# Squaring the half-angle sines on three engines instead of two, and four small evictions of VectorE moved

## What is computed

```
q, k, v = x @ Wq.T + bq, x @ Wk.T + bk, x @ Wv.T + bv       # 16 heads of 8
f(z)    = [cos(z @ proj / sqrt(8)), sin(z @ proj / sqrt(8))] / sqrt(128)
kv      = sum over tokens of f(k) * v                        # per head
x       = layernorm(x + (f(q) @ kv) @ Wo.T + bo)
p       = softmax(x @ Wr + br), the two largest kept and scaled to sum 1
x       = layernorm(x + sum over the two experts of p_e * (relu(x @ W1e + b1e) @ W2e + b2e))
```

## Time and profile before

| | |
|---|---|
| time, median of 3 runs | 525.64 us (525.46 to 525.82) |
| the profiled execution's own time | 526.61 us |
| its span, first to last instruction | 524.8 us |
| PE busy (matmul) | 475.4 us, 91% |
| DVE busy | 414.2 us, 79% |
| POOL busy | 393.5 us, 75% |
| ACT busy | 370.9 us, 71% |
| the chain that ended last | PE 64%, POOL 13%, issue 6%, DVE 6% |

### The profile page before, as it was taken

One profiled execution on the slowest core, in us unless ns is written; L12 is line 12 of the kernel. 1 busy time (PEld: TensorE's weight loads), 2 busy tenths in 40 slices (PEclk: granted clock), 3 DMA queues, 4 the chain that ended last, 5 costly groups with the idle time before them and its releaser, 6 DMA issues.

```text
span 524.8 us, 12192 instructions
## 1 busy us (share of the span) xinstructions
PE 475.4 (91%) x3739; PEld 277.5 (53%) x3739; DVE 414.2 (79%) x920; ACT 370.9 (71%) x505; POOL 393.5 (75%) x463
## 2 busy tenths in 40 slices
PE   5799999999999999999999998888999999999713
PEld 3343343343344344344344343338999989999701
DVE  4868979979979978988988887567678977777554
ACT  3797888797887888788788787585555555555235
POOL 2383398798888889889779779985777788687654
PEclk9999999999999999999999999899999999999957
DMA  4563154153154154143234221032222333222194
GB/s 102 174 201 122 27 156 126 56 161 122 45 157 162 37 146 153 39 137 137 67 116 141 62 62 47 1 82 58 63 64 73 89 108 94 65 80 59 36 326 156
DMA packets 44740, 53.94 MB, mean 103 GB/s; under 512 B 8563, under 2 KB 25237, under 8 KB 44677
## 3 DMA queue, kind: packets, MB, share of 16 engines
q1 hardware_dynamic: 39728, 43.82, 28.2%
q0 software_dynamic: 4320, 8.95, 5.1%
q10 hardware_dynamic: 628, 0.38, 0.3%
HBM read 33.09 MB, written 20.04 MB: 101 GB/s over the span
## 4 chain that ended last, share of the span: by engine, by line
PE 64%; POOL 13%; issue 6%; DVE 6%; DMA 3%; SPq 3%; ACT 2%; DVEq 0%; POOLq 0%; ACTq 0%
PE misc L643 11%; PE ang L795 10%; PE ang L804 10%; PE ang L592 8%; PE misc L612 7%; POOL rows_s L1489 5%; PE ang L579 5%; PE ang L584 5%; POOL feats L1464 3%; DVE turns L1077 2%; PE misc L531 1%; POOL rstd L1482 1%; ACT feats L883 1%; DMA feats<-expert_dram 1%; PE misc L658 1%
## 5 line engine op out<-in xcount | busy, mean ns | idle before, releaser
L1077 DVE TENSOR_SCALAR turns<-ang 128x1024 f16<-128x1024 f32 x128 | 156.1, 1220 | 44.2 <-PE ang L584 27.1
L882 ACT ACTIVATE feats<-ang 128x1024 f32<-128x1024 f32 x128 | 131.2, 1025 | 62.3 <-PE ang L592 61.6
L1464 POOL TENSOR_TENSOR feats<-feats 128x1024 f32<-128x1024 f32 x56 | 106.8, 1908 | 58.2 <-ACT feats L883 57.7
L883 ACT ACTIVATE feats<-ang 128x1024 f32<-128x1024 f32 x128 | 131.2, 1025 | 0.0
L1085 DVE TENSOR_TENSOR feats<-feats 128x1024 f32<-128x1024 f32 x72 | 92.8, 1289 | 0.6 <-ACT feats L883 0.6
L1633 POOL DMA_INDIRECT routed_dram<-rows_s,slots x64 | 76.2, 1190 | 18.9 <-issue 18.3
L1663 POOL DMA_INDIRECT expert_dram<-feats x71 | 69.9, 985 | 24.5 <-DVE feats L1388 15.5
L592 PE MATMUL ang<-turns,negi 128*128 128x512 f16 x256 | 77.8, 386 | 10.5 <-DVE turns L1077 10.4
L795 PE MATMUL ang<-feats 128*128 128x128 f32 x568 | 76.1, 277 | 3.9 <-DVE feats L1340 3.0
L953 ACT ACTIVATE feats<-experts 128x644 f32 x71 | 52.5, 739 | 34.2 <-DVE feats L1388 27.0
L804 PE MATMUL ang<-experts,feats 128*128 x568 | 75.6, 276 | 0.4 <-DVE feats L1348 0.4
(11 more groups left out here) (199 smaller groups left out, 551.6 us busy)
## 6 DMA issues: line engine op xcount, KB each, us to landing
stk<-parts_dram SPq DMA_DIRECT2D x126, 128.0 KB, 2.7
parts_dram<-parts SPq DMA_DIRECT2D x16, 512.0 KB, 3.2
feats<-routed_dram SPq DMA_DIRECT2D x72, 65.5 KB
experts<-ffn_W SPq DMA_DIRECT2D x16, 256.0 KB, 3.2
feats<-expert_dram SPq DMA_DIRECT2D x16, 256.0 KB, 5.3
out<-feats SPq DMA_DIRECT2D x8, 256.0 KB, 2.1
x_all<-attn_x SPq DMA_DIRECT2D x7, 256.0 KB, 5.1
expert_dram<-feats POOLq DMA_INDIRECT x71
```

The source lines that it names most:

```text
L882: act.activation(f[:, 0, :], a, ACT.Sin, scale=TWO_PI)
L883: act.activation(f[:, 1, :], a, ACT.Sin, scale=TWO_PI / 2).then_inc(s["sines"], 1)
L1077: dve.tensor_scalar(turns[:, u % 2, :], ang[:, slot(ph, u), :], MAGIC, -MAGIC, ALU.add, ALU.add)\
L1464: pool.tensor_tensor(f, f, f, ALU.mult).then_inc(s["sq_p"], 1)
```

## The change

Eight of the 16 squares of a sequence go to DVE (units 0, 2, 4, 5, 6, 10, 13, 15), four to POOL (1, 3, 8, 12) and four to ACT (7, 9, 11, 14). In the diff the first `square` is ACT's and the second DVE's. ACT squares unit `u - 1` behind the sines of unit `u`, so unit 7 in step 8, 9 in step 10, 11 in step 12 and 14 in step 15, with its activation function Square on `feats` in place. Units 4, 6 and 10 leave POOL for DVE; units 7, 9, 11 and 14 leave DVE for ACT. On DVE, `kv_evac` moves from the end of step 12 to just behind its rounding, and `take_ranks` and `move_base` follow it there, ahead of the square of unit 10. The list of POOL's scatters and PE's `ranks` are not touched by the diff.

```diff
-POOL_SQ = (1, 3, 4, 6, 8, 10, 12)
+POOL_SQ = (1, 3, 8, 12)
+ACT_SQ = (7, 9, 11, 14)
...
+DVE_SQ = tuple(u for u in range(UNITS) if u not in POOL_SQ + ACT_SQ)
...
-def before(u, pool):
+def before(u, whose):
 
-    return sum((x in POOL_SQ) == pool for x in range(u))
+    return sum(x in whose for x in range(u))
...
             def squared(b, u):
 
-                wait(pe, "sq_v", UNITS - len(POOL_SQ), b, before(u + 1, False))
-                wait(pe, "sq_p", len(POOL_SQ), b, before(u + 1, True))
+                wait(pe, "sq_v", len(DVE_SQ), b, before(u + 1, DVE_SQ))
+                wait(pe, "sq_p", len(POOL_SQ), b, before(u + 1, POOL_SQ))
+                wait(pe, "sq_a", len(ACT_SQ), b, before(u + 1, ACT_SQ))
...
+            def square(b, u):
+                if u % UNITS not in ACT_SQ:
+                    return
+                wait(act, "sines", UNITS, b, u + 1)
+                f = feats[:, u % HALF, 1, :]
+                act.activation(f, f, ACT.Square).then_inc(s["sq_a"], 1)
...
                     sines(b, ph, u)
+                    if not (first and u == 0):
+                        square(b, u - 1)
...
             def square(b, u):
-                if u % UNITS in POOL_SQ:
+                if u % UNITS not in DVE_SQ:
                     return
...
-            BEFORE_ROUND = ((6, moments), (10, take_logits), (13, move_base))
-            AFTER_ROUND = ((5, residual), (10, largest))
-            AFTER_SQUARE = ((5, statistics), (10, which), (12, take_ranks), (13, slot_numbers))
+            BEFORE_ROUND = ((6, moments), (10, take_logits))
+            AFTER_ROUND = ((5, residual), (10, largest), (12, take_ranks), (12, move_base))
+            AFTER_SQUARE = ((5, statistics), (10, which), (13, slot_numbers))
...
                     if u == 11:
                         kvT_evac(b)
+                    if u == 12:
+                        kv_evac(b)
...
-                    if u == 12:
-                        kv_evac(b)
```

More of the change, by code:

```diff
@@ L249, in build @@
             "raw_T", "raw_ev", "pad_ok", "setup", "sel_0", "sel_ok", "sel_mm", "sel_ev",
-            "angles", "rounded", "reduced", "sines", "sq_v", "sq_p",
+            "angles", "rounded", "reduced", "sines", "sq_v", "sq_p", "sq_a",
             "xT_mm", "xT_ev", "q_mm", "q_ev", "k_mm", "k_ev", "v_mm", "v_ev", "split", "parts_out",
@@ L940, in body @@
                     sines(b, ph, u)
+                    if not (first and u == 0):
+                        square(b, u - 1)
             sequences(body)
+            square(BATCH, -1)
             act.activation(warm[:, :], zero_t[:, :], ACT.Sigmoid)
```

## The result

The changed kernel takes **512.11 us** (median of 4 runs, 511.84 to 513.27) against 525.73 us of the kernel before in the same comparison (525.46 to 529.32, 4 runs): ratio 0.973, 95% interval 0.9685 to 0.9774, a gain of 13.6 us. Forecast were 514.6 us and a gain of 11.0, with a range of 511.5 to 520.5; the measured time lies 0.6 us inside its lower end.

A forecast was written before the change was run, and what follows sets the result against it. PE was taken to bound the middle sequences, with waits for DVE's roundings and POOL to win. Gains 0.9 (first) + 5.4 (middle) + 4.7 (last) = 11.0 us, from 525.64 to 514.6 us; range 511.5 to 520.5.

The forecast's parts named there:

- the first sequence: Step 12 of the first sequence: gain 0.9 us, its wait of 1.14 less 0.2 by which DVE's chain stays late.
- the middle ones: Six middle sequences: 0.9 us each from step 12, 5.4 in all; a middle sequence was to take 40.2 us.
- What can be won: Middle sequences: PE is the bound, so without less work for PE only its idle 1.12 us a sequence can be won.
- Step 12: With unit 9's square on ACT, DVE rounds unit 12 in time and PE's reduction starts earlier: 0.9 us a sequence.
- The walk of what is late next: Step 12 behind the rounding: kv_pad, slot_m and base were to be ready for the first product, with 0.15 us to spare.
- ACT at no cost: ACT's four squares at about 1.0 us each cost PE nothing; unit 11's sines, the tightest place, have 0.8 us to spare.
- The normalised rows: Steps 6 to 8: DVE's added square delays POOL's normalising, so PE's 0.25 us wait stays; bounds -0.3 and +0.4 a sequence.
- The exclusive port of the Trainium skill: DVE and POOL lock the shared port by whole instructions: squares of units 4 and 5 each stop L1489 1.2 us; 2.4 less gain.
- The last sequence: POOL's chain loses three squares, 5.7 us, less 1.0 taken for delay by DVE's squares: the end comes 4.7 us earlier.
- The end: At the change to Sigmoid, ACT's square of unit 14 is covered by the rows from memory: cost nothing, uncovered 1.0 once.
- No table is loaded for Square: Rival on ACT: a table load for each square, eight a sequence, 10.3 us, making the kernel some 580 us; chance 0.06.
- The wait did not move: Rival in step 12: kv_pad and base, or ACT's unit 11, become late instead; 6.3 us go, 520.9 us; chance 0.06.

The follow-up runs named there:

- run 2: The kernel before with the square of unit 9 alone moved from DVE to ACT, DVE's order as before: ratio 0.9793 to the kernel before.
- Runs 6: The changed kernel with DVE's step 12 as ranks, kv_pad, base; in the last sequence unit 14 on DVE and ACT's out before its second bias part: 509.86 us.
- run 8: The kernel before with DVE's new order in steps 12 and 13 alone, all squares as before: 527.29 us, ratio 1.0016.
- run 7: The changed kernel with 1.9 us more work on ACT (two unread copies) behind the square of unit 9 in every sequence: 522.71 us, ratio 0.9921.
- run 3: The kernel before with the squares of units 4 and 6 alone moved from POOL to DVE, order as before: ratio 0.9958 to the kernel before.
- run 4: The changed kernel with the square of unit 14 on DVE and not on ACT: ratio 0.9721 to the kernel before.
- run 1: The changed kernel with DVE's old order in steps 12 and 13: 546.85 us, ratio 1.0101 to the kernel before.

## Why the prediction was right, and where its sizes were off

The time was right and so was most of the mechanism: the waits that were named went, by the squares that were named. The terms were not. By the profiles the first sequence gave 0.3 us for 0.9, the middle ones 8.2 for 5.4 and the last one 5.9 for 4.7. The first of these lies in the start, which differs between executions, and it took 0.6 back from the other two; they alone would have put the time at the very edge of the range. So the time is inside it in part by luck.

- **What can be won.** "all that can be won there without less work for PE is its idle 1.12 us a sequence" was too low: 1.32 were won. A wait costs PE its idle and the overlap of the instructions on both sides of it (0.98 for an idle of 0.87, 0.32 for one of 0.25), and 0.16 stood under no idle that is listed.
- **Step 12.** Right in mechanism and size: 0.9 forecast, 0.96 by run 2, and it comes from the one square of unit 9. PE's wait for it is 0 where it was 0.87. The walk of what is late next had the right moves and an error of 0.13: "the order of these three moves with the rounding and costs nothing, with 0.15 us to spare". There was nothing to spare: the product starts 0.15 us behind base's end before (208.04, 208.19) and 0.14 behind it after (202.45, 202.59), so PE comes some 0.15 us behind base's end at the earliest, and the walk left this out. And in the new order kv_pad no longer stands between the ranks and base, which waits for them, and base ends 1.86 us behind the start of the rounding where it was 1.71; PE waits 0.11. Runs 6 and 8 show this from both sides (39.61 and 41.19).
- **ACT at no cost.** Right in the middle sequences: 1.08 us a square (1.0 taken), no wait of PE for it; 0.74 us to spare at unit 11's sines by run 7 where I had 0.8. Not at the end, see below.
- **The normalised rows.** This is the step that failed: "With a second beside them I add one more such delay, 0.7 to 1.2 us, and it uses up the 1.1. So the 0.25 us that PE waits for the rows stays." The delay was there but smaller: the four pieces took 4.43 us and not 3.92, 0.5 more, with a median of 1067 ns for 797. The start came 1.1 earlier, as said. So the wait went: 0.34 a sequence by run 3, of which 0.25 is idle and the rest the overlap that the wait had cost. With it goes a term that the forecast hasn't at all, the 0.16 at the reduction of unit 3. The rows' 0.32 and these 0.16, with 0.08 more than forecast from unit 12 and 0.13 less from base, are 0.43 a sequence, 2.6 us of the 2.8 that the middle's 5.4 lacked to 8.2. The exclusive port of the Trainium skill ("SBUF — State Buffer"), whole instruction by whole instruction, would have made both squares cost 1.2 and the sum 2.4 us less. The trace has single instructions that take about this much longer (a DVE square of 2.22 us in step 8, 2.73 in run 4), so the rule holds in kind, but which instructions meet has to be read, and here the second square cost 0.5.
- **The last sequence.** 4.7 forecast, 5.9 measured. "I take 1.0" for POOL's delay beside DVE's squares was the mis-sized term. From the square of unit 4 to `slots_of_picks` POOL's chain took 26.74 us (314.60 to 341.34); from where it now starts, at the normalising, it takes 20.27 (306.44 to 326.71). That is 6.5 less, where three squares are 5.6: the delays fell by 0.9 and did not grow by 1.0. Some instructions are longer now (by the changed kernel's lines, L1558 1.99 us for 1.03, L1585 1.32 for 0.39), others were before (by the old lines, L1545 1.53, now 0.52; L1569 1.29, now 0.22; L1616 1.19, now 0.21). This was not to be foreseen by the sum, and it is luck that it fell this way. Seen from PE it is the same: waits of 2.17, 0.85, 1.30 and 0.25 us and 1.7 of the clock went, 6.3 in all, and two new ones of 0.14 came. So `slots_of_picks` comes at 326.71, and PE's "about 1.2 us of the later wait" is 0, though DVE still waits 1.06 us for POOL:

```profile
327.20 0.22 DVE L1185 TENSOR_REDUCE slots<-slot_k 128x8 uint32<-128x64 f32 x1 [1.06 <-POOL slot_k L1640]
...
328.64 0.60 PE L596 MATMUL ang<-turns,negi 128*128 128x512 f16 x2
```

- **The end.** "I cost this at nothing; uncovered it would be 1.0 once" was wrong by 0.7. ACT is behind at the end (its sines of unit 13 on run back to back), the square of unit 14 stands ahead of the table load, and the first weights, which ACT hands over at 336.41, and not the rows from memory, release the first tile (the name in brackets is that of another wait of the same matmul, for a copy that had ended at 335.73). Run 4, without this square on ACT, has 0.12 us there and not 0.80:

```profile
333.11 1.16 ACT L895 ACTIVATE feats<-feats 128x1024 f32<-128x1024 f32 x1
334.29 1.28 ACT L958 ACT_TABLE_LOAD   x1
...
335.69 0.72 ACT L968 ACTIVATE feats<-experts 128x644 f32 x1
```

```profile
336.52 1.13 PE L800 MATMUL ang<-feats 128*128 128x128 f32 x8 [0.80 <-DVE feats L1355]
```

- **The first sequence.** 0.9 forecast; its wait in step 12 fell from 1.14 to 0.18, as said, but of these 0.96 the execution kept 0.3 (the wait for stk was 1.67 us, before 1.21, and a stretch of lower clock stands behind it that the kernel before has not).
- **The rivals.** No table is loaded for Square (two loads, as before); 32 squares stand among the 256 sines. So the list of the Trainium skill ("ScalarE: Activation LUTs", the part on table sets), which does not name it, was no sign against the change. The wait did not move in the middle sequences. It would have with the old order (run 1). In the last one PE waited 2.0 us for the picks when only two of POOL's squares left (run 3). The scatters were not touched, and nothing came of them.

## What to carry to other kernels

Where one engine is busy for 97% of a loop, a change gains little more than its idle time (here 1.32 us of 41.06, for an idle of 1.12), so list each of its waits with its place and ask for each which instruction of the late engine stands ahead of the one it waits for. Here one square in one step was 0.96 us a sequence, while two of the four squares moved to ACT were worth 0.12 together in a middle sequence (and 1.5 in the last). An engine's total slack says little: ACT had 2.5 us a sequence and 0.74 where it mattered, and DVE in run 4 had 3.7 and none in five steps on end. What a list of waits leaves out, the overlap beside a wait and a delay too short to show as idle, comes out when two timelines are laid side by side.

When work goes from an engine that is a chain (POOL in the last sequence), look at what stands behind it in its list before moving a part: with two squares alone gone (run 3) PE waited 2.0 us for the picks, with three gone (the change) 0.14.

## What the runs showed of the hardware

**An idle of PE and its clock.** In the last sequence four executions had a wait of PE of nearly one length. The granted clock behind it, by stretch (the kernel before: 0.72 in 328 to 334, after 2.17 us); run 8, after 2.16 us, and run 2, after 2.13:

```profile
331.00:337.00 6.00, 5.44 (x39) 2.17 (x40) 2.20 (x7) 2.31 (x3) 5.35 (x13) 0.72 0.00 0
...
319.00:329.00 10.00, 7.87 (x50) 2.95 (x49) 4.70 (x19) 4.93 (x6) 9.18 (x18) 0.66 0.00 0
```

and run 3, after 2.03 us:

```profile
333.00:340.00 7.00, 4.97 (x37) 1.85 (x37) 5.82 (x9) 4.64 (x5) 6.57 (x12) 1.00 0.01 2
```

So much the same wait was followed by the lower clock (1.2 of 2.4 GHz) for a stretch that cost 6 x 0.28 = 1.7 us of work at full speed, by one that cost 10 x 0.34 = 3.4, and by none. What a wait of this size costs behind itself can't be told from its length alone; taking it away, as the change does, also takes that away.

**DVE and POOL** are longer in single instructions where they run beside each other, in both directions: in the changed kernel a `128x128` tensor_scalar on POOL takes 0.78 to 1.47 us and the DVE square 1.21 to 2.29. The square's median of 1.22 hides it, and which instructions are hit differs from one schedule to the next, as the last sequence shows. That each is held up by the other is read from the timelines; no run here takes one of the two away.
